# Second attention: full and diagonal key blocks in turn

## The reference

```python
q = (h @ Wq).reshape(b, s, 16, 16)        # 16 query heads
k = (h @ Wk).reshape(b, s, 4, 16)         # 4 key heads, each serves 4 query heads
v = (h @ Wv).reshape(b, s, 4, 16)
q, k = rope(q), rope(k)
scores = einsum('bqhd,bkhd->bhqk', q, k) / 4
scores = where(causal, scores, -inf)
attn = softmax(scores)
ctx = einsum('bhqk,bkhd->bqhd', attn, v)
```

## Time and profile before

| | |
|---|---|
| median of 3 runs | 3288.45 us (3288.26 to 3292.18) |
| the profiled execution's own time | 3290.54 us |
| its span in the trace | 3288.7 us |
| TensorE, VectorE, ScalarE, GpSimd busy | 87%, 66%, 51%, 54% |
| mean granted TensorE clock | 0.951 |

### The profile page before, as it was taken

The page is one execution under the profiler, slowest core; times in us unless marked ns, Lnnn a source line. Parts: engine busy times, 40 slices in busy tenths (PEclk is TensorE's granted clock), DMA queues, the critical chain, the costliest instruction groups (busy, mean ns, idle before and its releaser), DMA issues. The chain is left out here.

```text
span 3288.7 us, 53958 instructions
## 1 busy us (share of the span) xinstructions
PE 2870.1 (87%) x17348; PEld 1696.3 (52%) x17349; DVE 2156.6 (66%) x4620; ACT 1672.2 (51%) x3836; POOL 1766.0 (54%) x2330
## 2 busy tenths in 40 slices
PE   5677899899899989989988998988879999999990
PEld 3454545545555555554555554444346666666660
DVE  5767887897888888888788888757432222222226
ACT  2344566667657657666765765765512222222224
POOL 6886656766765775775676585241232222222225
PEclk8778999999999999999999999999889999999995
DMA  1000000000000000000000000001333333333325
GB/s 47 4 14 9 10 9 16 16 21 19 21 27 11 28 20 16 26 19 21 19 21 26 13 26 17 14 24 59 129 93 58 51 58 59 58 53 58 58 44 207
DMA packets 101517, 123.20 MB, mean 37 GB/s; under 512 B 14256, under 2 KB 90032, under 8 KB 100272
## 3 DMA queue, kind: packets, MB, share of 16 engines
q1 hardware_dynamic: 74992, 85.01, 8.5%
q0 software_dynamic: 25728, 34.88, 6.2%
q10 hardware_dynamic: 576, 0.53, 0.0%
HBM read 58.23 MB, written 61.36 MB: 36 GB/s over the span
## 5 line engine op out<-in xcount | busy, mean ns | idle before, releaser
L909 ACT ACTIVATE wd<-SP_ 128x512 f32<-128x512 f32 (+3 forms) x1536 | 723.2, 488 | 478.8 <-PE SP_ L1595 338.1
L1211 DVE TENSOR_REDUCE NM<-MX 128x1 f32<-128x512 f32 (+3 forms) x1216 | 763.2, 655 | 245.0 <-PE MX L1552 146.6
L1549 PE MATMUL MX<-KST,QST 96*128 96x512 bf16 (+3 forms) x1536 | 454.3, 333 | 102.6 <-DVE NM L1211 89.6
L572 POOL TENSOR_TENSOR wg<-wu 128x1024 f32<-128x1024 f32 x256 | 487.7, 1926 | 85.9 <-DVE wu L1047 85.7
L1781 POOL DMA_INDIRECT scratch_h<-Y,XG x136 | 212.3, 1561 | 594.6 <-DVE Y L1844 501.3
L1592 PE MATMUL SP_<-QST,KST 99*128 99x512 bf16 (+3 forms) x1536 | 500.9, 333 | 34.9 <-ACT wd L909 14.7
L1822 DVE TENSOR_TENSOR AG<-UB,SL 128x512 f32<-128x512 f32 x136 | 94.1, 692 | 464.8 <-PE UB L1861 464.8
L1799 ACT ACTIVATE SL<-GB 128x512 f32<-128x512 f32 x136 | 81.3, 598 | 603.0 <-PE GB L1861 603.0
L1060 DVE TENSOR_TENSOR wg<-wu,SUM 128x1024 f32<-128x1024 f32 x256 | 309.7, 1212 | 83.1 <-PE SUM L1446 83.1
L1549 PEld LDWEIGHTS MX<-KST,QST 96*128 96x128 bf16 x1536 | 135.0, 97 | 432.8 <-DVE NM L1211 299.0
L1609 PE MATMUL OA<-wd,V 128*32 128x512 f32 (+3 forms) x3072 | 335.0, 509 | 1.1 <-ACT wd L909 0.4
(11 more groups left out here) (246 smaller groups left out, 4999.7 us busy)
## 6 DMA issues: line engine op xcount, KB each, us to landing
XG<-scratch_xs SPq DMA_DIRECT2D x136, 130.0 KB, 2.1
wu<-in_L_attn_x SPq DMA_DIRECT2D x64, 128.0 KB, 2.1
scratch_x<-wu SPq DMA_DIRECT2D x64, 128.0 KB, 1.7
scratch_h<-H SPq DMA_DIRECT2D x64, 128.0 KB, 1.7
X<-scratch_x SPq DMA_DIRECT2D x16, 512.0 KB, 4.0
out<-X SPq DMA_DIRECT2D x16, 512.0 KB, 2.9
wg<-in_L_ffn_Wg SPq DMA_DIRECT2D x8, 512.0 KB
wu<-in_L_ffn_Wu SPq DMA_DIRECT2D x8, 512.0 KB
```

Of the source, the lines that this page charges most:

```text
L572: sg["prod1"].by(pool.tensor_tensor(P1[:, k // 2, (k % 2) * hh * D:(k % 2 + 1) * hh * D].rearrange("p (h e d) -> p h e d", h=hh, e=HD), QK ...
L909: sg["exp"].by(act.activation(PR[:, n % 8, q0:512], SP_[:, n % 2, q0:512], ACT.Exp))
L1211: sg["mx"].by(dve.tensor_reduce(NM[:, u % 2, part, i, h:h + heads], MX[:, index % 2, 0:heads * n].rearrange("p (h n) -> p h n", n=n), AX.X ...
L1549: m = pe.matmul(out[:, k], QST[0:MROW, j % 2, g * G + h + k, i * P:(i + 1) * P], KST[0:MROW, keys % RK, g, 0:n], start=k == 0, stop=not la ...
```

## The change

`steps()` is the order of (unit, key block) that ScalarE and TensorE both follow. For an even chunk it stays 0, 1, 2, 3. For an odd chunk it was 0 to 7, four full blocks and then four diagonal ones; it becomes 0, 4, 1, 5, 2, 6, 3, 7. The first block is still the one that starts the accumulation and the last the one that ends it. `max_plan`, `FIRST_STEP` and all semaphore counts go by step number and are unchanged.

```diff
@@ -247,9 +247,11 @@
             FIRST_STEP.append(FIRST_STEP[-1] + length(u))
         assert FIRST_STEP[-1] == NSTEPS
 
+        WOVEN = [kt + part for kt in range(CH) for part in (0, CH)]
+
         def steps():
             for u in range(NU):
-                for kt in range(length(u)):
+                for kt in (range(CH) if length(u) == CH else WOVEN):
                     yield u, kt
 
         def last_step(j):
```

## The result

The changed kernel takes 3302.52 us (median of 19 runs, 3298.32 to 3306.86), the kernel before 3292.17 us on the same chips (19 runs, 3288.21 to 3300.55). The ratio is 1.0029, interval 1.0022 to 1.0035: +9.5 us by the ratio, +10.4 by the two medians, where +9.1 was forecast. As a time 3297.5 was forecast, 5.0 us less than measured; 3.7 of these lie in the base, since the forecast started from 3288.45, the median of three executions. The profiled execution took 3302.52 us with a span of 3300.6, 11.9 us more than before, at a mean granted clock of 0.948 (0.951).

The account below looks back on a forecast made before the run. No engine is full: VectorE bounds steps 2 to 4 of a unit, TensorE steps 5 to 7 and 0. Four units sum to +1.3 us a chunk, seven chunks to +9.1: 3297.5 us from 3288.45, range 3283 to 3307.

Parts of the forecast that it names:

- Two regimes: Within a unit, VectorE is never idle in steps 2 to 4, TensorE never in steps 5 to 7 and 0.
- the hand-overs: Step 4, TensorE's last wait for VectorE (0.72 us), and step 1, VectorE's wait for TensorE (0.61 us); only TensorE's changes between count.
- TensorE's prices: From start distances: 512-column score 0.22 us, mask 0.06, values product 0.21 per 128 columns; +0.25 in unit 37's full stretch.
- Unit 36, +0.5: First unit of the chunk: 0.25 us on TensorE plus 0.30 lost waiting for step 6's exponential, taken as +0.5.
- ScalarE's part: In step 6, 0.84 us more exponential work delays step 7's first score, losing the 0.30 us TensorE had gained.
- Unit 37, +0.4: Second unit: +0.25 us on TensorE, +0.15 from step 7's second score waiting for step 6's last exponential.
- Unit 38, +0.5: Third unit: gains of steps 4 to 6 vanish in step 7's BR wait; values +0.42 and masks +0.12 us remain.
- Unit 39, -0.1: Fourth unit: no VectorE waits from step 4, so -0.27 us counts, against up to +0.26 in steps 1 to 3.
- Seven chunks of +1.3, the eighth nothing: Odd chunks: seven at +1.3 us make +9.1; the last, with holes on every engine, counted as nothing, between -3 and +3.
- rival 1: ScalarE's extra work in step 6 is absorbed: +0.7 us or less a chunk, +2 to +6 in all; chance 0.35.
- rival 3: ScalarE becomes the bound of step 6 in three units of four: +26 us, 3314; chance 0.08.
- rival 2: Alternating wide and narrow steps spares TensorE most of 10.7 us of waits for exponentials: 3279 us; chance 0.12.

Follow-up runs that it names:

- cut_values2: The kernel before, with the values product of step 2 of the odd chunks cut to 256 of its 512 columns: 3281.57 us, ratio 0.9971.
- cut_values4: The kernel before, with the values product of step 4 of the odd chunks cut to 256 of its 512 columns: 3280.99 us, ratio 0.9966.
- narrow_exp6: The changed kernel, with the exponentials of step 6 of the odd chunks taken of 256 columns instead of 512: 3290.8 us in one execution.
- late_wide: The changed kernel with block order 0, 6, 5, 4, 1, 2, 3, 7 in odd chunks: 3312.8 us, ratio 1.0067 to the kernel before.
- tail_only: The changed kernel with block order 0, 1, 4, 5, 2, 6, 3, 7 in odd chunks: 3304.91 us in one execution.
- plan_later: The kernel before, with VectorE's maxima work of odd chunks (key heads 1 to 3) moved within each unit by up to half a step: 3333.45 us, ratio 1.0113.
- plan_later_rows: The kernel before, with maxima moved by up to half a step and the transposes of their rows 0.9 of a step later: 3322.76 us, ratio 1.0086.

## Why the prediction was right, point by point

- **Two regimes, and a unit's length set by TensorE between the hand-overs.** Shown: the same 0.42 us of TensorE work counts 0.07 us in step 2 of unit 37 and 0.43 in step 4's product (cut_values2, cut_values4), and the wait in step 4 of unit 37 grew from 0.72 to 1.05 where 1.1 was named.
- **TensorE's prices.** Shown: a mask and 128 columns of a score, priced at 0.11, took 0.12 us with them in unit 37 (1.68 to 1.56), and the values product, priced at 0.42, took 0.42 to 0.46 off each of the four units when it was cut. By the Trainium skill, page "TensorE: Matmul & The Clock Gate", section "Back-to-back issue gap" (81 ns for 128 columns, 131 ns for 512), the TensorE sum of such a unit would be about nothing, an estimate. This case's trace doesn't agree: a score of 512 columns takes 0.22 us (1571.29 to 1571.51), and the sum by spacings came out within 0.01 of unit 37's growth. The 0.12 alone would not tell the two apart, since the page's pair gives about 0.10 for it, an estimate too.
- **Unit 36, +0.5.** It grew by 0.64: +0.10 by the start of step 2, then no gain up to the first score of step 7, which needs ScalarE (34.44 to 34.65 us after the start, +0.21, that is the 0.10 and 0.11 more), then +0.43 of values. ScalarE's part, forecast 0.30, measured 0.27 by narrow_exp6.
- **Unit 37, +0.4.** It grew by 0.27. The missing 0.14 is a wait for an exponential that the kernel before had in step 6 and that the narrower step 5 removed. The forecast overlooked it: it does not stand in the idle column, only in the distance between two starts.
- **Unit 38, +0.5.** It grew by 0.58, and its gains went into a wait for VectorE, as forecast. The wait was another one: LG, some 3.7 us ahead of it (0.42 to 0.92), and not BR, which shrank from 1.09 to 0.91.
- **Unit 39, -0.1: the step that failed.** It grew by 0.15. "There are no waits for VectorE from step 4 on, so everything counts" left out ScalarE, which was priced for units 36 and 37 only. TensorE's terms, if anything, understated the gain: with narrow exponentials the unit is 0.26 shorter than before, near the lower bound of -0.3. ScalarE took 0.41 of it back.
- **Seven chunks of +1.3, the eighth nothing.** The size per chunk was 1.65: +0.25 more than forecast in unit 39, +0.14 in unit 36 and +0.08 in unit 38, less 0.13 in unit 37. Seven chunks gave 9.6 - 3.5 and the eighth +2.9, and the even chunks gave +4.3. That the total came out near +9.1 is luck to that extent; the forecast had none of these terms.
- **The seventh odd chunk, -3.5.** It holds units 52 to 55, where VectorE has holes. 2.3 of the 3.5 us lie in unit 55, whose granted clock is 0.95 in the kernel before and 1.00 in the changed one (TensorE busy 28.72 and 27.25 us with the same 198 records). In all five kernels with one of the new orders and unchanged widths the unit has 1.00 and 30.3 to 31.1 us; in all others it has 0.85 to 0.95 and 31.8 to 34.3. The other 1.2 us lie in units 52 to 54 at about the same clock, and their cause stays open.

**The rivals.** Hidden (rival 1): refuted, narrow_exp6 shows that ScalarE's part is paid in three units of four, and a steady chunk grew by 1.65, not 0.7. ScalarE as the full bound of step 6 (rival 3): refuted, at most 0.41 of 0.84 is paid, and no unit of the steady chunks grew by 1 us. Faster by fewer waits for exponentials (rival 2): TensorE's idle time before its 512-column scores, by shape in the changed kernel, is

```profile
L1594 PE MATMUL SP_<-QST,KST 99*128 99x512 bf16 x750 | 286.3, 388 | 25.3 <-DMA QST<-MR 10.5 <-ACT wd L911 10.5
```

10.5 us for ScalarE where it was 10.7: the waits that weaving was to spare are all still there.

**The last unit.** In the last odd chunk (110.97 us, 108.07 in the earlier trace rows) the loss lies in its last unit. The window of that unit in the kernel before, then in the changed kernel:

```profile
2339.68:2363.95 24.27, 19.12 (x125) 6.21 (x125) 1.50 (x6) 16.21 (x37) 9.19 (x11) 0.93 0.53 180
```

```profile
2348.21:2375.76 27.55, 21.30 (x125) 6.82 (x125) 1.59 (x6) 16.15 (x37) 9.15 (x11) 0.81 0.47 158
```

The same 125 records of TensorE take 2.18 us more of the 3.28, at a granted clock of 0.81 where it was 0.93. The length of this unit follows the clock over the fourteen kernels of this case: 22.3 to 22.9 us at 1.00, 23.8 to 24.6 at 0.93, 26.9 at 0.87, 27.3 and 27.6 at 0.81, 28.0 at 0.76, 28.9 at 0.74, 29.7 (late_wide) at 0.71. tail_only, whose steps 5 to 7 are those of the changed kernel, has 24.6: so the loss doesn't belong to the wide late steps as such. What brings the clock down there stays open. One row of ScalarE's timeline there, in the changed kernel:

```profile
2360.86 0.49 ACT L911 ACTIVATE wd<-SP_ 128x384 f32<-128x384 f32 x1 [2.80 <-remote]
```

The profile names no engine for this hole of 2.80 us, and the kernel before has one of its own on TensorE (1.99 us at 2353.01, put down to issue). The orders tried move this chunk by +1.4 to +5.9 us. No run separates hole and clock.

## What to carry to other kernels

Where two engines take turns as the bound, an equal exchange of work is not neutral: work of TensorE that moves from VectorE's stretch into its own is paid in full, and the room that it leaves in VectorE's stretch only lengthens a wait there. So find the hand-overs (TensorE's last wait for VectorE, VectorE's first for TensorE), price only what crosses them, and keep TensorE's narrow steps in TensorE's stretch. Then price the second engine (here ScalarE) in every unit of the pattern, and take waits from distances between starts, since overlapped matmuls hid 0.14 and 0.17 us of them from the idle column. And before work is planned anew on one engine, look at what a third one is doing at that time: here 16 columns on VectorE, put beside a long product on GpSimd, took 1.62 us instead of 0.17.

## What the runs showed of the hardware

In the even chunks, whose order of blocks the change does not touch, 13 of the 32 units move by 0.8 to 1.9 us, in both directions, and the others by 0.24 or less. One such place is in unit 34, which takes 32.78 us in the changed kernel at a granted clock of 0.90, and 30.92 at 0.94 before. TensorE's timeline in the changed kernel:

```profile
1456.32 0.39 PE L1551 MATMUL MX<-KST,QST 96*128 96x512 bf16 x1 [0.85 <-DVE MR L1238]
...
1457.68 0.61 PE L1531 MATMUL SUM<-BR,below 128*128 128x32 f32 x2 [0.97 <-DVE LG L1140]
...
1460.15 3.68 PE L1439 MATMUL SUM<-ident,wg 128*128 128x128 f32 x16 [0.48 <-DVE BR L1191]
```

The granted clock there, from the table of windows (the column ahead of the last two):

```profile
1456.00:1458.00 2.00, 0.71 (x3) 0.45 (x3) 2.00 (x6) 0.77 (x2) 2.00 (x2) 0.77 0.00 0
1458.00:1460.10 2.10, 1.67 (x9) 1.02 (x8) 1.85 (x14) 0.55 (x2) 0.05 (x1) 0.50 0.00 0
```

And the same 16 transposes before, with the table's row for the time ahead of them:

```profile
1453.66 1.97 PE L1437 MATMUL SUM<-ident,wg 128*128 128x128 f32 x16 [0.90 <-DVE BR L1189]
```

```profile
1451.70:1453.60 1.90, 1.06 (x9) 0.70 (x9) 1.66 (x12) 0.55 (x2) 0.00 (x0) 1.00 0.00 0
```

TensorE was busy 0.71 us of two in the changed kernel, behind a wait for MR that the kernel before didn't have; the clock fell to its 1.2 GHz level and the transposes took 3.68 us instead of 1.97. The kernel before is not free of such falls. It has a shorter one some 9 us earlier in the same unit: four products of the hidden layer (L1466) take 1.91 us at 1445.00, at a granted clock of 0.51, and 1.02 in the changed kernel. So a fall moves from place to place within a unit, and the unit with more time at the lower level is the longer one, as in the last unit and in unit 55 above. That is where totals of kernels here differ by several us more, or less, than their steady units do (+4.3 us in the even chunks of the changed kernel, -4.0 in those of cut_values2 and narrow_exp6). Such a difference isn't shown to be an effect of the edit's own work, and no experiment here holds it fixed.

The other thing is the hold of VectorE by GpSimd: 24 cases in plan_later and plan_later_rows, in which 16 columns took 1.10 to 1.63 us instead of 0.17, each ending 0.03 us after the product over 1,024 columns (L579) that ran beside it.
